# Windowed attention and a ternary FFN on one core: projections as two list steps, scores and maxima at places of their own

## The chip, the cores and the metric

One core of one Trainium2 chip. The metric is the device time of one execution of the whole kernel, in microseconds. TensorE is called PE, VectorE DVE, ScalarE ACT, GpSimd POOL and SyncE SP, as in the profile.

## The reference

A post-layernorm transformer layer over x of 16 x 512 x 256 (16 batch rows of 512 tokens), in float32:

```
qkv  = x @ Wqkv + bqkv                      16 heads of 16, blocks of 128 tokens
attn = softmax(q k^T / 16) v                each block sees itself and its neighbours, |kpos - qpos| <= 128
x1   = layernorm(x + attn @ Wout + bout)
Wq   = clip(round(W / (mean|W| + 1e-5)), -1, 1)       for W1 and W2
out  = layernorm(x1 + relu(x1 @ Wq1^T + b1) @ Wq2^T + b2)
```

## The kernel before, in words

The sixteen batch rows run through a software pipeline. `steps` (L209) calls each engine's `step` for row after row; while the attention of row b runs, the layer's second half (`POST`: ot, op, ln1, x1, x1t, f1, f2, ln2) of row b - 1 and the projections (qk, vp) of row b + 1 run beside it. Each row has four quads v of four heads. The order of the work is written out by hand: `SIDE[v]` (L54) is the list of side steps of quad v, and every engine walks it in that order, doing its part of each step.

- Attention comes in units, twelve of scores and twelve of maxima a quad (three for each head: blocks 1, 2, and 3 with 0). A score unit (`scores`, L504) is one or two matmuls of 384 or 2 x 256 columns into one of two banks `st`; ACT's `exp` (L765) reads it. A maxima unit (`max_scores`, L526) computes the same scores the other way round, for the quad two further on, into one of two banks `mx`; DVE's `row_max` (L923) reads it. Score units of quads 0 and 1 and maxima units of quads 2 and 3 use the lower 64 rows of PE's array, the others the upper 64, so that a score unit and a maxima unit can run side by side.
- `weave` (L108) sets where the units lie: two score and two maxima units in turn (s, m, s, m) make a run, six runs a quad, at one place inside a side step. Places are counted by `COST` (columns, places).
- Every projection and transposition has two halves (`in_halves`, L544; `transposes_in_halves`, L568): in the first, the array's lower rows write bank 0 and the upper ones bank 1 of a pair, then they swap. Before the second half PE waits on `s_half` until the first is complete. `passed` issues the units of a place.
- Side steps use two bank pairs in turn (`pairs`, L92). Before it writes, `pair_free` (L499) waits for the last reader: hid_lo of DVE after an f1 step, v_next of ACT after vp, DVE's addition (L1026) after f2, ACT's copy u (L825) after pv.
- nmt transposes the negated maxima (L603) for the next quad, pv (L613) multiplies the masked probabilities by v, ut (L626) transposes the result. POOL masks the probabilities (`mask`, L1091, four instructions after exp 5 and after exp 11), and pv of the next quad waits for it.
- `warm` (L490) issues matmuls whose results nobody reads ahead of some steps (`WARM`; `WARM_END` for the last row of the pipeline), each time a pair of 512 columns.
- ACT does its part of nmt, ot, pv and x1t ahead of the exps of that step, of all others behind them (L865 to L874). DVE follows `dve_order` (L184), in which `LAG` puts some parts behind later maxima.
- SP issues all transfers in the order of `TRANSFERS` (L76): a stack is six DMAs of 128 KB that lay out q and k (hi and lo parts) of a quad, x is the transposed input two rows on, residual the plain one, maxima the negated maxima, store half a result.

The lines of the helpers: L522 scores, L538 maxima, L563 all projections, L494 warm pairs, L583 ot and x1t, L960 qk_lo, L981 oT_lo, L1014 x1T_lo, L1019 hid_lo, L843 x1, L849 x1T_hi.

## Time and profile before

| | us |
|---|---|
| median of 3 runs | 1104.79 (1100.22 to 1110.8) |
| the profiled execution | 1103.1 |
| its span, first to last instruction | 1101.4 |
| PE busy in it | 997.7 |
| DVE busy in it | 846.3 |
| ACT, POOL busy in it | 621.7, 552.7 |
| mean granted clock of TensorE | 0.961 |

All durations come from one profiled execution; its time is 0.15% under the median of the runs, and the time outside the span is 1.7 us. PE's busy time is the union of modelled matmul intervals (a 512-column matmul shows about 0.4 us, and the next may start 0.23 us after it), so that starts are the better measure of how fast PE goes on. A clock of 1.00 means 2.4 GHz.

### The profile page before, as it was taken

How to read it: one execution, taken by the hardware profiler on the slowest of the kernel's cores; microseconds unless marked ns; L12 is line 12 of the kernel's file. 1: busy time of each engine (PE TensorE's matmuls, PEld its weight loads, DVE VectorE, ACT ScalarE, POOL GpSimd, SP SyncE). 2: the span in 40 equal slices, each digit the busy share in tenths (PEclk: the TensorE clock that was granted, in tenths of full speed). 3: DMA queues.
4: the chain of work that ended last, by engine and by line, in shares of the span. 5: the costliest groups of instructions: out<-in, count | busy, mean ns of one | idle time of the engine just before them, and what ended most of it. 6: DMA issues, size and time to landing. Idle time of an engine off the chain costs nothing.

```text
span 1101.4 us, 30158 instructions
## 1 busy us (share of the span) xinstructions
PE 997.7 (91%) x11408; PEld 780.5 (71%) x11408; DVE 846.3 (77%) x2965; ACT 621.7 (56%) x1275; POOL 552.7 (50%) x904
## 2 busy tenths in 40 slices
PE   5688998999999999999999899999999899998966
PEld 4465776777778677777778687777778677766755
DVE  3876888878798888879798887879788887867223
ACT  2355665747475565747476565747566574746411
POOL 2376355364645456374645456374655446354520
PEclk8678999999999999999999999999999999998988
DMA  5846435455364536556264536546254635541000
GB/s 115 162 68 82 60 63 97 67 90 86 54 97 69 88 55 95 77 80 97 41 103 66 96 51 98 79 74 103 42 97 67 97 56 79 79 68 33 11 11 20
DMA packets 57024, 81.92 MB, mean 74 GB/s; under 512 B 7712, under 2 KB 27696, under 8 KB 56880
## 3 DMA queue, kind: packets, MB, share of 16 engines
q1 hardware_dynamic: 56880, 80.00, 46.1%
q8 instruction: 91, 1.49, 0.7%
q14 instruction: 53, 0.43, 0.2%
HBM read 20.20 MB, written 8.39 MB: 26 GB/s over the span
## 4 chain that ended last, share of the span: by engine, by line
PE 60%; DVE 18%; ACT 9%; issue 7%; POOL 4%; DMA 1%; SPq 0%; DVEq 0%; POOLq 0%; ACTq 0%
PE shared L563 28%; PE shared L613 11%; PE st L522 9%; DVE mx L933 8%; PE mx L538 6%; ACT probs L780 4%; PE shared L494 2%; ACT x L843 2%; DVE hid_lo L1019 2%; PE shared L583 2%; ACT oT_x1T_hi L849 2%; DVE rmax L933 1%; POOL probs L1099 1%; DVE qk_lo L960 1%; POOL probs L1103 1%
## 5 line engine op out<-in xcount | busy, mean ns | idle before, releaser
L933 DVE CUSTOM_DVE_ANT_0 mx<-mx,band 128x384 f32<-128x384 f32 (+1 forms) x1024 | 478.8, 518 | 151.1 <-PE mx L538 145.9
L780 ACT ACTIVATE probs<-st 128x384 f32<-128x384 f32 (+1 forms) x768 | 365.1, 526 | 173.1 <-PE st L522 171.3
L1099 POOL TENSOR_SCALAR_AFFINE_SELECT probs<-probs 128x512 f32<-128x512 f32 (+1 forms) x256 | 127.4, 522 | 406.6 <-ACT probs L780 406.6
L538 PE MATMUL mx<-k_stack,q_stack 48*128 48x384 f32 (+1 forms) x1024 | 269.5, 344 | 14.8 <-DVE rmax L933 8.5
L522 PE MATMUL st<-q_stack,k_stack 50*128 50x384 f32 (+1 forms) x1024 | 243.9, 333 | 10.2 <-ACT probs L780 4.9
L522 PEld LDWEIGHTS st<-q_stack,k_stack 50*128 50x128 f32 x1024 | 167.7, 189 | 58.8 <-issue 31.0
L538 PEld LDWEIGHTS mx<-k_stack,q_stack 48*128 48x128 f32 x1024 | 170.1, 191 | 40.3 <-DVE rmax L933 27.3
L613 PE MATMUL shared<-probs,v_aug 128*32 128x384 f32 (+1 forms) x2048 | 164.9, 447 | 9.4 <-POOL probs L1103 7.2
L563 PE MATMUL shared<-w2q,hid_hi 64*128 64x256 f32 x1024 | 144.5, 290 | 0.3
L933 DVE DVE_READ_ACCUMULATOR2_ANT rmax<- 128x1 f32 x1024 | 144.6, 141 | 0.0
L563 PE MATMUL shared<-w2q,hid_lo 64*128 64x256 f32 x1024 | 136.0, 278 | 0.0
L613 PEld LDWEIGHTS shared<-probs,v_aug 128*32 128x32 f32 x2048 | 90.8, 112 | 56.4 <-issue 18.4
L1103 POOL TENSOR_SCALAR_AFFINE_SELECT probs<-probs 128x512 f32<-128x512 f32 (+1 forms) x256 | 127.1, 521 | 0.0
L563 PEld LDWEIGHTS shared<-w2q,hid_hi 64*128 64x128 f32 x1024 | 115.7, 185 | 2.0 <-PE shared L563 0.6
L563 PEld LDWEIGHTS shared<-w2q,hid_lo 64*128 64x128 f32 x1024 | 116.8, 185 | 0.0
L563 PE MATMUL shared<-oT_x1T_hi,w1q 64*128 64x512 f32 x512 | 112.3, 407 | 0.3
L563 PE MATMUL shared<-oT_x1T_lo,w1q 64*128 64x512 f32 x512 | 109.9, 400 | 0.0
L1019 DVE SCALAR_TENSOR_TENSOR hid_lo<-shared,hid_hi 128x512 fp32r<-128x512 f32 x128 | 82.1, 682 | 31.8 <-ACT hid_hi L856 31.8
L494 PE MATMUL shared<-wqkv_hi 64*128 64x512 f32 x596 | 95.2, 416 | 8.1 <-DVE qk_lo L960 4.4
L825 ACT ACTIVATE u<-shared 128x512 f32<-128x512 f32 x64 | 38.0, 594 | 101.9 <-PE shared L613 101.8
L856 ACT ACTIVATE hid_hi<-shared 128x512 fp32r<-128x512 f32 x128 | 69.6, 595 | 30.8 <-PE shared L563 30.4
L1169 POOL TENSOR_SCALAR x<-x,ln_mv,ln_rstd 128x256 f32<-128x256 f32 x60 | 73.3, 1227 | 3.2
(113 smaller groups left out, 1848.7 us busy)
## 6 DMA issues: line engine op xcount, KB each, us to landing
q_stack<-qk_hi SPq DMA_DIRECT2D x128, 128.0 KB, 4.0
k_stack<-qk_hi SPq DMA_DIRECT2D x128, 128.0 KB, 4.9
x_raw<-in_xT SPq DMA_DIRECT2D x16, 512.0 KB, 5.9
q_stack<-qk_lo SPq DMA_DIRECT2D x64, 128.0 KB, 5.6
k_stack<-qk_lo SPq DMA_DIRECT2D x64, 128.0 KB, 5.8
y<-in_x SPq DMA_DIRECT2D x16, 512.0 KB, 6.2
out<-x SPq DMA_DIRECT2D x32, 256.0 KB, 2.4
probs<-in_w2T SPq DMA_DIRECT2D x1, 1024.0 KB, 10.2
```

The costliest lines, as they stand in the source:

```text
L494: pe.matmul(out[i][:, 0:width], WQKV[0][rows, 0, 0:P], WQKV[0][rows, 1, 0:width], start=True, stop=True)
L522: mm = pe.matmul(PST[i % N_SCORE][:, col:col + n], SK[rows, hd, W * m:W * m + W], SQ[rows, hd, q0:q0 + n], start=True, stop=True)
L538: mm = pe.matmul(PMX[i % N_MAX][:, col:col + n], SQ[rows, hd, W * m:W * m + W], SK[rows, hd, k0:k0 + n], start=True, stop=True)
L563: mm = pe.matmul(out[k][:, cols], lhs(rows), rhs(rows), start=(swap == 0 and n == 0 and bias is None), stop=(swap == 1 and n == count - 1) ...
L613: mm = pe.matmul(out[0][32 * g:32 * g + 32, q0:q0 + width], VAUG[:, vq, m, g, :], PR[:, vq % 2, g // 2, lo:lo + width], start=(m == 0), st ...
L780: act.activation(PR[:, v % 2, g // 2, lo:lo + n], PST[i % N_SCORE][:, 0:n], ACT.Exp, scale=SCALE) \
L856: act.activation(HID[0][:, f, :], PG[:, 2 * k + i, :], ACT.Relu).then_inc(s_hh, 1)
L933: mx = dve.tensor_tensor_reduce(ps, ps, band, 1.0, -3e38, ALU.add, ALU.max, RMAX[:, g, m:m + 1])
L1019: dve.scalar_tensor_tensor(HID[1][:, f, :], PG[:, 2 * k + i, :], 0.0, HID[0][:, f, :].bitcast(F32), ALU.max, ALU.subtract).then_inc(s_hl, 1)
L1099: pool.affine_select(out=pr_before, in_=pr_before, compare_op=ALU.is_ge, fill=0.0, base=0, pattern=[[0, n], [1, W]], channel_multiplier=-1)
L1103: last = pool.affine_select(out=pr_after, in_=pr_after, compare_op=ALU.is_ge, fill=0.0, base=0, pattern=[[0, n], [-1, W]], channel_multipl ...
L1169: pool.tensor_scalar(X1[:, t, :], X1[:, t, :], MV2[:, t, 0:1], RS2[:, t:t + 1], ALU.subtract, ALU.mult).then_inc(s_o, 1)
```

## The change

Each step that works in halves stands twice in `SIDE`: `("start", step)` is its first half, the step's own name the second. The evacuations on ACT and DVE belong to the second. Both stand next to each other everywhere, so the matmuls of a step are the same as before. The lists differ otherwise in three places: vp stands ahead of f1 1, `("ut", 2)` behind xs and `("ut", 3)` at the end of quad 3, and x1 1 stands behind pv. Every score unit and every maxima unit has a position of its own (`SCORES_AT`, `MAXIMA_AT`, in thousandths of the quad's cost, pv counted as 5200 columns instead of 2500). Units at one place are issued scores first, then maxima. By these tables the units lie at 13, 11, 9 and 10 places of the four quads, where there were 6 in each.

ACT gets lags like DVE's: x1t's part comes behind the exps of its step. DVE's op lag is 2 (0 before), which leaves its order as it was. Two warm pairs are added ahead of `("start", "qk", 0)`; in the last row x1t has 16 instead of 14 and f1 0 none instead of 8. The wait of a quad's first score unit for the stack of the quad two further on goes, the wait of that quad's first maxima unit for it stays. `TRANSFERS` has another order. `pairs` now hands the two bank pairs out in turn by their use. `steps` runs one turn more, in which no step has a row.

The diff, cut to its core:

```diff
-    ["nmt", "pv", "ut", "ot", "op", ("ln1", 0), ("ln1", 1), ("ln1", 2), ("ln1", 3)],
-    [("qk", 0), ("x1", 0), ("x1", 1), "nmt", "pv", ("x1", 2), "ut", ("x1", 3), "x1t", ("qk", 1), ("f1", 0)],
-    [("f1", 1), "vp", ("f1", 2), ("f1", 3), "nmt", "pv", "ut", ("xs", 0), ("xs", 1)],
-    [("f2", 0), ("ln2", 0), "xr", ("ln2", 1), "nmt", "pv", "ut", ("f2", 1), ("ln2", 2), ("ln2", 3)],
+    ["nmt", "pv", ("ut", 0), ("start", "ot"), "ot", ("start", "op"), "op", ("ln1", 0), ("ln1", 1), ("ln1", 2),
+     ("ln1", 3)],
+    [("start", "qk", 0), ("qk", 0), ("x1", 0), "nmt", "pv", ("x1", 1), ("ut", 1), ("x1", 2), ("x1", 3),
+     ("start", "x1t"), "x1t", ("start", "qk", 1), ("qk", 1), ("start", "f1", 0), ("f1", 0)],
+    [("start", "vp"), "vp", ("start", "f1", 1), ("f1", 1), ("start", "f1", 2), ("f1", 2), ("start", "f1", 3),
+     ("f1", 3), "nmt", "pv", ("xs", 0), ("xs", 1), ("ut", 2)],
+    [("start", "f2", 0), ("f2", 0), ("ln2", 0), "xr", ("ln2", 1), "nmt", "pv", ("start", "f2", 1), ("f2", 1),
+     ("ln2", 2), ("ln2", 3), ("ut", 3)],
 ]
 
-COST = {"qk": (6144, 12), "vp": (6144, 24), "op": (6144, 24), "ot": (1024, 8), "x1t": (1024, 8), "ut": (512, 4),
-        "f1": (4096, 8), "f2": (8192, 32), "nmt": (0, 0), "pv": (2500, 1)}
+HALF_COST = {"qk": (3072, 6), "vp": (3072, 12), "op": (3072, 12), "ot": (512, 4), "x1t": (512, 4),
+             "f1": (2048, 4), "f2": (4096, 16)}
+COST = {"ut": (512, 4), "nmt": (0, 0), "pv": (5200, 1)}
...
-HALVED = {"qk", "vp", "op", "ot", "x1t", "f1", "f2"}
...
-RUN = 2
-RUNS_AT = (0.95, 0.93)
-TRANSFERS = (('stack', 3), ('maxima', 0), ('x', 0), ('stack', 0), ('maxima', 1), ('stack', 1), ('residual', 0), ('maxima', 2), ('maxima', 3), ('stack', 2), ('store', 0), ('store', 1))
-
-LAG = {"ln1": 3, "ln2": 0, "qk": 0, "ut": 0, "ot": 1, "x1t": 0, "f1": 0, "op": 0, "f2": 0}
+SCORES_AT = ((201.86, 241.86, 488.2, 488.2, 572.67, 572.67, 631.93, 691.93, 771.43, 771.43, 930.43, 930.43),
+             (168.94, 168.94, 370.2, 378.2, 537.72, 562.72, 701.04, 726.04, 789.62, 814.62, 922.49, 922.49),
+             (47.43000000000001, 87.43, 279.19, 384.19, 400.22, 400.22, 511.54999999999995, 526.55, 681.2, 681.2, 871.11, 871.11),
+             (191.17, 191.17, 245.68, 245.68, 513.4100000000001, 520.4100000000001, 690.22, 698.22, 820.42, 860.42, 928.28, 936.28))
+MAXIMA_AT = ((161.86, 216.86, 448.2, 463.2, 532.67, 540.67, 591.93, 651.93, 731.43, 791.43, 890.43, 938.43),
+             (143.94, 143.94, 338.2, 370.2, 529.72, 529.72, 693.04, 726.04, 789.62, 814.62, 922.49, 922.49),
+             (47.43000000000001, 87.43, 279.19, 384.19, 400.22, 415.22, 511.54999999999995, 526.55, 681.2, 681.2, 911.11, 919.11),
+             (191.17, 231.17, 285.68, 285.68, 545.4100000000001, 553.4100000000001, 690.22, 698.22, 820.42, 860.42, 928.28, 936.28))
+TRANSFERS = (("maxima", 0), ("stack", 3), ("maxima", 1), ("x", 0), ("stack", 0), ("stack", 1), ("residual", 0),
+             ("maxima", 2), ("stack", 2), ("maxima", 3), ("store", 0), ("store", 1))
+DVE_LAG = {"ln1": 3, "ln2": 0, "qk": 0, "ut": 0, "ot": 1, "x1t": 0, "f1": 0, "op": 2, "f2": 0, "vp": 0}
+WARM = {("start", "ot"): 4, ("start", "op"): 4, ("ut", 0): 2, ("ut", 1): 2, ("ut", 2): 2, ("ut", 3): 2,
+        ("start", "x1t"): 2, ("start", "qk", 0): 2}
+WARM_END = {("start", "x1t"): 16}
+WARM_UP = 14
+FILLED = set()
+ACT_LAG = {"nmt": -1, "ot": -1, "pv": -1, "x1t": 0, ("ut", 0): -1, ("ln2", 1): 0, ("ln1", 3): -1, ("x1", 3): 0}
 N_PAIRS = 2
-WARM_END = {"x1t": 14, ("f1", 0): 8}
-WARM_UP = 14
-WARM = {"ot": 4, "op": 4, "ut": 2, "x1t": 2}
...
-        total = sum(COST.get(name_of(s), (0, 0))[0] for s in SIDE[v])
-        at, starts = 0, []
-        for s in SIDE[v]:
-            starts.append(at)
-            at += COST.get(name_of(s), (0, 0))[0]
-        place, last = {}, -1
-        runs = range(0, UNITS, RUN)
-        where = [(i + RUNS_AT[0] * RUN) / UNITS * total * RUNS_AT[1] for i in runs]
-        for k, s in enumerate(SIDE[v]):
-            if name_of(s) in HALVED:
-                cost, places = COST[name_of(s)]
-                middle = starts[k] + cost / 2
-                free = [n for n in range(last + 1, len(where))]
-                if free:
-                    last = min(free, key=lambda n: abs(where[n] - middle))
-                    place[last] = (k, places // 2)
-        slot = [[] for _ in SIDE[v]]
-        for n, i in enumerate(runs):
-            if n in place:
-                k, p = place[n]
-            else:
-                k = max(k for k, s in enumerate(SIDE[v]) if starts[k] <= where[n] and COST.get(name_of(s), (0, 0))[0])
-                cost, places = COST[name_of(SIDE[v][k])]
-                p = min(int((where[n] - starts[k]) / cost * places), places - 1)
-            slot[k] += [(p, kind, u) for u in range(i, i + RUN) for kind in ("scores", "max")]
-        out.append(slot)
-        order = [u for units in slot for _, kind, u in units if kind == "max"]
-        assert order == list(range(UNITS))
+        costs = [cost_of(s) for s in SIDE[v]]
+        starts = [sum(c for c, _ in costs[:k]) for k in range(len(costs))]
+        total = sum(c for c, _ in costs)
+        put = {}
+        for kind, table in (("scores", SCORES_AT), ("max", MAXIMA_AT)):
+            for i in range(UNITS):
+                pos = table[v][i] * total / 1000
+                k = max(k for k in range(len(costs)) if costs[k][0] and (starts[k] <= pos or k == 0))
+                put[kind, i] = (k, min(int((pos - starts[k]) / costs[k][0] * costs[k][1]), costs[k][1] - 1))
+            for k, s in enumerate(SIDE[v]):
+                if name_of(s) in HALF_COST and (k, 0) not in [put[kind, i] for i in range(UNITS)]:
+                    near = sorted(range(UNITS), key=lambda i: abs(table[v][i] * total / 1000 - starts[k]))[0]
+                    if abs(table[v][near] * total / 1000 - starts[k]) <= 1300 and \
+                            all(put[kind, i] <= (k, 0) for i in range(near)) and \
+                            all(put[kind, i] >= (k, 0) for i in range(near + 1, UNITS)):
+                        put[kind, near] = (k, 0)
+        out.append([sorted(((p, kind, i) for (kind, i), (k, p) in put.items() if k == n), key=lambda u: (u[0], u[1] != "scores", u[2]))
+                    for n in range(len(costs))])
+        for kind in ("scores", "max"):
+            assert [i for units in out[-1] for _, what, i in units if what == kind] == list(range(UNITS))
...
+def turn_of(v, step):
...
+    if name == "nmt":
+        return (0, v + 1) if v < 3 else (1, 0)
+    turn = v if name == "pv" else step[1]
+    return (-1, (turn - 1) % QUADS) if turn == 0 or turn > v else (0, turn - 1)
...
+def act_order(v):
+    out, late, exps = [], [], 0
+    def due(now):
+        while late and late[0][0] <= now:
+            out.append(("side", late.pop(0)[1]))
+    for step, woven in zip(SIDE[v], WOVEN[v]):
+        lag = lag_of(ACT_LAG, step)
+        if lag < 0:
+            due(UNITS + 100)
+            out.append(("side", step))
+        for _, kind, i in woven:
+            if kind == "scores":
+                out.append(("exp", i))
+                exps += 1
+                due(exps)
+        if lag >= 0:
+            late.append((exps + lag, step))
+            due(exps)
+    due(UNITS + 100)
+    return out
...
-                    pe.wait_ge(s_nmin[v], 16 * b + 16)
-                    if v < 2 or stages(at)[2]:
-                        pe.wait_ge(s_stk[(v + 2) % 4], 96 * (b + v // 2) + 96)
...
+            def exchange(passed):
+                passed()
+                pe.wait_ge(s_half, halves[0])
+            def one_half(out, terms, filled, passed, second, ready=None, bias=None):
 
 
                 count = len(terms[0])
-                if bias is not None:
+                if second:
+                    exchange(passed)
+                elif bias is not None:
                     for k, rows in enumerate((LOWER, UPPER)):
                         pe.matmul(out[k][:, :], bias(rows), ONES_R[rows, :], start=True, stop=False, skip_group_check=True)
-                for swap in range(2):
-                    if swap:
+                for n in range(count):
+                    if n > 0 or not second:
                         passed()
-                        halves[0] += 2
-                        pe.wait_ge(s_half, halves[0])
-                    for n in range(count):
-                        if n > 0 or not swap:
-                            passed()
-                        if ready is not None and not swap:
-                            ready(n)
-                        for rows, k in ((LOWER, swap), (UPPER, 1 - swap)):
-                            cols, lhs, rhs = terms[k][n]
-                            mm = pe.matmul(out[k][:, cols], lhs(rows), rhs(rows), start=(swap == 0 and n == 0 and bias is None),
-                                           stop=(swap == 1 and n == count - 1), skip_group_check=True)
-                            if n == count - 1:
-                                mm.then_inc(filled if swap else s_half, 1)
-
-            def transposes_in_halves(out, block, filled, passed, ready=None):
-
-
-                for swap in range(2):
-                    if swap:
+                    if ready is not None and not second:
+                        ready(n)
+                    for rows, k in ((LOWER, second), (UPPER, 1 - second)):
+                        cols, lhs, rhs = terms[k][n]
+                        mm = pe.matmul(out[k][:, cols], lhs(rows), rhs(rows), start=n == 0 and not second and bias is None,
+                                       stop=n == count - 1 and bool(second), skip_group_check=True)
+                        if n == count - 1:
+                            mm.then_inc(filled if second else s_half, 1)
+                            halves[0] += not second
...
-                    for step, woven in zip(SIDE[v], WOVEN[v]):
-                        row = row_of(v, step, at)
-                        before = name_of(step) in ("nmt", "ot", "pv", "x1t")
-                        if row is not None and before:
-                            side_work(v, step, b, *row, at)
-                        for _, kind, i in woven:
-                            if kind == "scores" and attn:
-                                exp(b, v, i, at)
-                        if row is not None and not before:
-                            side_work(v, step, b, *row, at)
+                    for kind, what in act_order(v):
+                        if kind == "exp":
+                            if attn:
+                                exp(b, v, what, at)
+                        else:
+                            row = row_of(v, what, at)
+                            if row is not None:
+                                side_work(v, what, b, *row, at)
```

## Rows read from the trace of the kernel before

**Rows 1.** The page's busy table: busy us, share of the span, instructions
```profile
PE 997.7 (91%) x11408; PEld 780.5 (71%) x11408; DVE 846.3 (77%) x2965; ACT 621.7 (56%) x1275; POOL 552.7 (50%) x904
```

**Rows 2.** Windows: stretch and its us, busy us of each engine (instructions), clock, DMA, GB/s
```profile
482.45:544.77 62.32, 58.71 (x708) 46.59 (x708) 51.80 (x185) 38.25 (x79) 33.19 (x56) 1.00 0.52 79
...
1049.00:1101.00 52.00, 36.00 (x328) 27.79 (x324) 16.52 (x39) 8.88 (x16) 6.70 (x14) 0.81 0.05 16
```

**Rows 3.** Waits over the span: who <- for whom, us in total, times, longest
```profile
PE shared L603 <- DVE neg_max L944: 15.6, 16, 1.9
...
PEld shared L563 <- DVE hid_lo L1019: 13.5, 14, 1.0
```

**Rows 4.** Timeline of DVE and PE around vp: start, us, idle before <- releaser
```profile
511.57 1.41 DVE L960 SCALAR_TENSOR_TENSOR qk_lo<-shared,bqk,qk_hi 128x512 fp32r<-128x512 f32 x2 [0.16 <-ACT qk_hi L804]
...
514.94 1.27 DVE L1019 SCALAR_TENSOR_TENSOR hid_lo<-shared,hid_hi 128x512 fp32r<-128x512 f32 x2
...
515.34 0.40 PE L563 MATMUL shared<-oT_x1T_lo,w1q 64*128 64x512 f32 x2
516.27 0.39 PE L563 MATMUL shared<-wqkv_hi,xT_hi 64*128 64x256 f32 x2 [0.53 <-DVE hid_lo L1019]
```

**Rows 5.** Timeline of PE: quad 3's ut, then the start of a row
```profile
475.05 0.63 PE L494 MATMUL shared<-wqkv_hi 64*128 64x512 f32 x4
475.52 0.41 PE L626 MATMUL shared<-identity,u 64*128 64x64 f32 x8
475.73 0.37 PE L563 MATMUL shared<-w2q,hid_hi 64*128 64x256 f32 x2
...
482.45 0.41 PE L603 MATMUL shared<-identity,neg_max 128*32 128x128 f32 x2 [0.94 <-DVE neg_max L944]
483.37 0.96 PE L613 MATMUL shared<-probs,v_aug 128*32 128x256 f32 x12 [0.51 <-POOL probs L1103]
```

**Rows 6.** Timeline of DVE and POOL in the same stretch
```profile
482.32 0.68 DVE L1026 TENSOR_TENSOR x<-shared,x 128x512 f32<-128x512 f32 x1
...
481.38 0.99 POOL L1099 TENSOR_SCALAR_AFFINE_SELECT probs<-probs 128x512 f32<-128x512 f32 x2 [1.88 <-ACT probs L780]
```

**Rows 7.** Timeline of ACT and PE around x1t and qk 1
```profile
506.31 1.09 ACT L849 ACTIVATE oT_x1T_hi<-shared 128x512 fp32r<-128x512 f32 x2 [1.11 <-PE shared L583]
...
507.84 0.44 PE L522 MATMUL st<-q_stack,k_stack 50*128 50x384 f32 x1
...
508.33 0.44 PE L522 MATMUL st<-q_stack,k_stack 50*128 50x384 f32 x1
```

**Rows 8.** Windows: the stretch from oT_lo on; timeline of PE at ut 1
```profile
490.19:505.05 14.86, 13.72 (x162) 10.84 (x160) 14.17 (x53) 10.65 (x23) 6.48 (x16) 1.00 0.71 106
...
503.44 0.73 PE L494 MATMUL shared<-wqkv_hi 64*128 64x512 f32 x4 [0.32 <-DVE qk_lo L960]
```

**Rows 9.** Timeline of ACT: x1 2 and x1 3
```profile
504.13 1.07 ACT L843 ACTIVATE x<-y,ln_neg_mean_rstd,ln_rstd 128x256 f32<-128x256 f32 x2
```

**Rows 10.** Timeline of PE: a run of units in f1 0; op's end
```profile
511.32 0.42 PE L563 MATMUL shared<-oT_x1T_lo,w1q 64*128 64x512 f32 x2
...
511.97 0.43 PE L563 MATMUL shared<-oT_x1T_hi,w1q 64*128 64x512 f32 x2
...
496.49 0.39 PE L563 MATMUL shared<-xT_hi,wqkv_hi 64*128 64x512 f32 x1
496.60 0.28 PE L563 MATMUL shared<-wout_lo,oT_x1T_hi 64*128 64x256 f32 x1
```

**Rows 11.** Timeline of SP's queue; DMA issues: count, KB each, us to landing
```profile
501.39 1.20 SPq L420 DMA_DIRECT2D q_stack<-qk_hi  x2
...
x_raw<-in_xT SPq DMA_DIRECT2D x16, 512.0 KB, 5.9
...
k_stack<-qk_lo SPq DMA_DIRECT2D x64, 128.0 KB, 5.8
```

**Rows 12.** Timeline of PE in the tail: f1 0's warm pairs
```profile
1067.74 3.58 PE L494 MATMUL shared<-wqkv_hi 64*128 64x512 f32 x16 [2.04 <-DVE oT_x1T_lo L1014]
```

More of the change, by code:

```diff
@@ L181, in max_quad, with lag_of @@
     return (1, v - 2) if nxt else None
+def lag_of(lags, step):
+    return lags.get(step, lags.get(name_of(step), 0))
 def dve_order(v):
@@ L192, in dve_order @@
     for step, woven in zip(SIDE[v], WOVEN[v]):
-        while late and (any(name_of(s) == NEEDS.get(name_of(step)) for _, s in late)
-                        or name_of(step) in USES_BANKS and sum(name_of(s) in USES_BANKS for _, s in late) >= N_PAIRS):
+        while late and (any(name_of(s) == NEEDS.get(name_of(whole(step))) for _, s in late)
+                        or name_of(whole(step)) in USES_BANKS and sum(name_of(s) in USES_BANKS for _, s in late) >= N_PAIRS):
             out.append(("side", late.pop(0)[1]))
@@ L202, in dve_order @@
         after = late[-1][0] + 1 if late and name_of(late[-1][1]) == name_of(step) == "ln2" else 0
-        late.append((max(maxima + LAG.get(name_of(step), 0), after), step))
+        late.append((max(maxima + lag_of(DVE_LAG, step), after), step))
         due(maxima)
@@ L206, in dve_order @@
     return out
+def act_order(v):
[18 more added lines that the diff above has]
+    return out
 def steps(step):
[L211 removed]
+    for row in range(-2, B + 2):
         step(row, row)
@@ new lines, in half_of_transposes @@
+            def half_of_transposes(out, block, filled, passed, second, ready=None):
+                if second:
+                    exchange(passed)
+                for t in range(TB):
+                    if t > 0 or not second:
+                        passed()
+                    if ready is not None and not second:
+                        ready(t)
+                    for rows, k in ((LOWER, second), (UPPER, 1 - second)):
+                        col = P * t + rows.start
+                        mm = pe.transpose(out[k][:, col:col + 64], block(rows, t, k), IDN[rows, rows])
+                        if t == TB - 1:
+                            mm.then_inc(filled if second else s_half, 1)
+                            halves[0] += not second
@@ L591, in side_work @@
             def side_work(v, step, b, dr, vq, at, passed):
+                second = int(name_of(step) != "start")
+                k = PAIR[at, v, step]
+                whole_step = step
+                step = whole(step)
                 name = name_of(step)
@@ L631, in side_work @@
                     c = step[1]
-                    if c == 0:
+                    if c == 0 and not second:
                         pe.wait_ge(s_xh, 2 * r + 2)
@@ L646, in side_work @@
                     left, right, col = (XT, WQKV, 2 * D) if name == "vp" else (OT, WOUT, 0)
-                    if first:
+                    if first and not second:
                         pe.wait_ge(s_wsplit_h, 2 if name == "vp" else 3)
@@ L675, in side_work @@
                     p = step[1]
-                    if first and p == 0:
+                    if first and p == 0 and not second:
                         pe.wait_ge(s_quant_d, 3)
@@ L735, in step @@
                         row = row_of(v, step, at)
-                        if row is not None and name_of(step) in COST:
+                        if row is not None and cost_of(step) != (0, 0) or row is not None and step == "nmt":
                             side_work(v, step, b, *row, at, passed)
+                        elif row is None and (at == 0 or at == -1 and v > 1) and name_of(whole(step)) in FILLED:
+                            cost, count = HALF_COST[name_of(whole(step))]
+                            out = pair_free(PAIR[at, v, step], b)
+                            for _ in range(count):
+                                passed()
+                                warm(out, 1, cost // count // 2)
                         units(1000)
@@ L786, in side_work @@
                 first = at is not None and at + dr == 0
-                k = PAIR.get((v, step))
+                k = PAIR.get((at, v, step))
                 if name == "xs":
@@ L950, in side_work @@
                 first = at is not None and at + dr == 0
-                k = PAIR.get((v, step))
+                k = PAIR.get((at, v, step))
                 if step == ("xs", 1) and first:
```

141 lines of the change are left out of this document (76 added, 65 removed).

## The prediction

> **What bounds the kernel now.** I read the page's busy table first, then one steady batch row cut out by windows, then the table of waits, and last the instructions of each engine around the longest waits. PE is busy 997.7 us, DVE 846.3 us [rows 1]. The kernel does the same thing sixteen times: the negated-maxima transposes that open a row start at 482.45 and again 62.32 us later. In that stretch PE is busy 58.71 us and DVE 51.80 us at a granted clock of 1.00; the last 52 us of the span have a clock of 0.81 [rows 2]. So the row period is PE's, with DVE at 83% close behind. The reader should see that "busy" hides waits on PE: a step's few long stalls come from one partner at a time. The table of waits gives them, each about once a row: the negated maxima's transposes wait for DVE (15.6 us in all, 16 times) and weight loads of side work for DVE's hid_lo (13.5 us, 14 times) [rows 3].
>
> **The change, part by part.** Matmuls, evacuations and masks are the same in number. What moves is their order, and where the 96 units a row (48 of scores, 48 of maxima) lie. I cost each per row and multiply by 15 rows that have a full partner.
>
> *vp before f1 1 (quad 2).* Today two f1 steps follow each other, and vp, third, needs the bank pair of f1 0. DVE reads that pair (hid_lo) only from 514.94 to 516.2, behind the maxima. PE's last f1 pair starts at 515.34, a 512-column pair takes 0.23 us, vp starts at 516.27: 0.70 us lost [rows 4]. Afterwards vp stands first and needs qk 1's pair, which DVE leaves at 512.98 (two instructions from 511.57, 1.41 us) [rows 4], just before f1 0 ends at about 513.0; f1 1 then needs f1 0's pair at 516.2, when vp (24 pairs of 0.115 us and two runs of units, 3.2 us) ends, so 0.1 us stays. What is late next is DVE: f1 1 now holds four maxima units (0.5 to 0.8 us each) before its evacuation, three f1 steps follow closely, and f1 3 waits for f1 1's. Placing DVE's durations one behind the other I get hid_lo at about 521.3 against f1 3's turn at 521.6: level. I take -0.6 (ends: -0.9, if the shorter bank waits of f1 2 go too; 0, if f1 3 or the maxima's banks take the wait over).
>
> *ut 3 behind f2 1 (quad 3).* Today, behind pv, two warm pairs (475.05, 0.47 us until ut) and ut (0.21 us) stand on PE before f2 1 at 475.73: 0.68 us. At the row's end PE idles: 0.94 us before the transposes at 482.45 and 0.51 us before pv at 483.37 [rows 5]. The new place is inside that idle time. But two things follow it. The last score units go from place 10 to 11 and 12 of the half (a place is 0.115 us), so the last exp, the four masks (from 481.38, 0.99 us for each two) and pv come 0.23 us later. And the transposes now share their bank pair with f2 1, so they queue behind DVE's addition at 482.32 (0.68 us) instead of ahead of it: ready at about 483.1 rather than 482.4, still 0.3 us before the masks allow pv [rows 5, 6]. Gain 0.68 - 0.23 = 0.45. I take -0.45 (ends -0.68 and 0; the latter if DVE's maxima run 0.5 us later than now).
>
> *ScalarE's x1T evacuation behind exp 4; units of qk 1 on own places.* Today ScalarE takes x1T (506.31, 1.09 us) before the exps of the units in the same step, and qk 1's next score units find both banks full: s6 starts at 507.84, s7 at 508.33, where 384 columns at 2.4 GHz (0.16 us) would separate them [rows 7]: 0.33 us lost, and I estimate as much ahead of s6. But the maxima there wait for DVE too (x1T_lo). Half goes: -0.3 (ends -0.6, 0).
>
> *x1 1 behind pv, and two warm pairs before qk 0.* DVE works without a pause from oT_lo (490.19) past qk_lo, to 505.05: 14.17 us busy in 14.86; ut's warm pairs start at 503.44, after 0.32 us idle that qk_lo ends [rows 8]. Four maxima now stand nearer to op's start, DVE begins them up to 0.2 us earlier and loses 0.2 of the 0.7 us that it idles there, so ut 1 can come 0.4 us sooner. Against it, ScalarE has three x1 left (0.55 each) behind exp 3 where it had two (504.13, 1.07 us) [rows 9], so x1t's last transposes come 0.5 us later, less what the two maxima units in x1t's first half cover. The new warm pairs cost 0.47 us on PE by [rows 5], below nothing only if they keep a clock that is at 1.00 already. They lie in a stretch where DVE is the slower: they eat slack first. Together I take +0.15 (ends -0.4, +0.9).
>
> *Forty-three places instead of twenty-four.* A run of 896 columns (0.37 us at 2.4 GHz) between two 512-column pairs makes start-to-start 0.65 us (511.32 to 511.97) where 0.23 + 0.37 is 0.60: 0.05 us a place [rows 10]. Nineteen more places cost up to 0.95. Today each score unit runs beside its maxima unit, on the other half of the array's rows; now many stand alone and rely on the two halves drifting apart. That they do drift: qk 0's first matmul starts at 496.49, before the last wout_lo one at 496.60, which stands ahead of it in the program [rows 10]. So I take +0.3 (ends 0, +0.95 without the loss of the rival below).
> The Trainium skill (TensorE: Matmul & The Clock Gate, Part 3) says matmuls start and end strictly in program order, "strict FIFO, no reordering". The trace's 0.11 us the wrong way round is against it. By the page the row would gain about 1.6 us from eight places alone, by the trace none of that.
>
> *SyncE's order and the removed wait.* Nothing on PE waits for a stack in a steady row, so the removed wait is worth 0. Moving x ahead of stack 0 is not free: stack 0's six DMAs are issued from 501.39 on, 0.6 us each, and the last kind lands 5.8 us after issue; x lands in 5.9 [rows 11]. Behind maxima 1 and x they start at about 503.6; the last is issued at 506.7 and lands at 512.5 or somewhat later; vp's first maxima unit wants it at 513.2. I take 0 (ends 0, +3).
>
> *Tail.* Eight warm pairs of f1 0 go, two come to x1t. Sixteen matmuls, they took 3.58 us in the tail, behind 2.04 us of idle time [rows 12]: at 0.45 us a pair that is the lower clock level, and without them the steps behind would run part of that time at that level. -1 (ends -3.4, +2).
>
> Sum: -0.6 - 0.45 - 0.3 + 0.15 + 0.3 = -0.9 a row; a further -0.1 for op's maxima, which no longer starve DVE, makes -1.0; times 15 is -15, tail -1: -16. The profiled execution took 1103.1 us (span 1101.4), 1.7 under the shown median of 1104.8, well inside the shown runs. 1103.1 - 16 = 1087.
>
> **Rivals.** *(A) More goes.* If PE's short bank waits shrink as well (PE's busy time counts them: at s6 and s7 alone they are 0.6 us), the lower ends of the first three parts hold: -2.2 a row, 1069. For it: every quad has two exps and two maxima in a run against two banks each. Against: DVE needs 51.8 of 62.3 us whatever the order. Chance 0.17.
> *(B) Given back.* The stall of vp turns up at f1 3 or ut 2, since DVE's work in quad 2 is unchanged and only bunched: first part 0, sum -0.4 a row, 1097 to 1103, say 1099. For it: four maxima units in f1 1. Chance 0.19.
> *(C) Lost side-by-side running (slower).* Eight places put two score units before two maxima units. If the second pair can't start until the last score matmul has, the first unit (0.16 to 0.27 us, say 0.2) is paid each time, 1.6 us, and single units on the lower rows hold both halves, about 0.9: -1.0 + 2.5 = +1.5 a row, 1103 + 22 = 1125. It decides from 1.0 us a row, five of the eight places. The page's rule is this rival; the pair at 496.49 speaks against it. Chance 0.08.
> *(D) Stack 0 late (slower).* If x and the stack transfer one after the other in full, the last landing is 514.6 or later, 1.4 us and more behind vp's unit; at 2.6 us a row: 1103 + 15 x 1.6 = 1127. It decides from a landing 1.0 us after 513.2. Against: the 5.8 us already hold the queueing of a sixth DMA behind five. Chance 0.06.
>
> **How the numbers follow.** Forecast -1.0 a row: 0.50, between 1078 and 1096. With A 0.17, B 0.19, C 0.08, D 0.06. Range 1068 to 1107: it takes in A to its middle and B, and leaves C and D out, and half of A's far side. A measurement tells about 1% (11 us) from no change. Faster by over 1% (under 1093.7): 0.47 of the forecast's, A's 0.17, 0.02 of B's: 0.66. Within: 0.03 + 0.16 + 0.01 = 0.20. Slower: C and D with 0.01 of B: 0.14.
>
> **What would show it.** Row period 61.3 us between transposes of quad 0 (62.32 now). No wait of vp for hid_lo, at most 0.1 us at f1 1. f2 1 right behind pv's units; idle before pv of quad 0 down by some 0.2 us with ut 3 in front. s7 behind s6 by under 0.2 us in qk 1. PE busy up by 0.4 us a row for the warm pairs. Wrong if k_stack appears as a releaser of mx (D); if score runs followed by maxima runs start one behind the other (C); if hid_lo or v_next releases f1 3 or ut 2 for over 0.4 us (B).

## The result and the profile after

The changed kernel takes 1162.3 us (median of 4 runs, 1155.6 to 1173.0) against 1102.5 for the one before: ratio 1.0503, 95% interval [1.0444, 1.0562]. It is slower by 5%. Forecast were 1087 and faster; the case that came true is rival D, stack 0 late, to which I had given a chance of 0.06 and 1127 us. The profiled execution is the slowest of the four (1173.0, mean granted clock 0.931; the others 0.939 to 0.941), so its rows hold some more loss of clock than the median execution, and the ratio is that of the other three.

The page of the changed kernel, its head and its chain (shares of the span):

```profile
span 1171.3 us, 30226 instructions
...
PE 1050.6 (90%) x11460; PEld 836.8 (71%) x11460; DVE 859.3 (73%) x2965; ACT 631.8 (54%) x1275; POOL 552.6 (47%) x904
...
PEclk8576999998998989999999999999899999999987
...
PE 63%; DMA 13%; DVE 11%; SPq 5%; issue 4%; ACT 3%; POOL 0%; DVEq 0%; POOLq 0%; ACTq 0%
PE shared L645 32%; DMA k_stack<-qk_lo 12%; PE shared L698 10%; PE st L601 8%; PE mx L617 8%; DVE mx L1023 5%; SPq L500 4%; PE shared L576 1%; PE shared L688 1%; PE shared L637 1%; PE shared L663 1%; DVE rmax L1023 1%; DVE oT_x1T_lo L1071 1%; DVE x L1116 1%; ACT oT_x1T_hi L926 1%
```

PE's share hardly moved (91% in [rows 1]), and would tell nothing. The chain does: one kind of DMA, k_stack<-qk_lo, holds 12% of the span. The table of waits says who waits for it, and how often (who <- for whom, us in total, times, longest):

```profile
PEld mx L617 <- DMA k_stack<-qk_lo: 47.6, 16, 4.6
...
PE mx L617 <- DMA k_stack<-qk_lo: 43.2, 16, 4.3
...
PEld shared L688 <- DVE x L1116: 19.0, 14, 1.5
```

Sixteen times, once a row. One of them in the timelines of SP's queue and of PE (start, us, idle before <- releaser):

```profile
543.73 0.66 SPq L544 DMA_DIRECT2D q_stack<-neg_maxT  x1
544.43 0.41 SPq L531 DMA_DIRECT2D x_raw<-in_xT  x1
544.94 1.21 SPq L500 DMA_DIRECT2D q_stack<-qk_hi  x2
546.19 1.25 SPq L500 DMA_DIRECT2D k_stack<-qk_hi  x2
547.48 0.60 SPq L500 DMA_DIRECT2D q_stack<-qk_lo  x1
548.12 0.63 SPq L500 DMA_DIRECT2D k_stack<-qk_lo  x1
...
555.05 0.34 PE L601 MATMUL st<-q_stack,k_stack 50*128 50x384 f32 x1
558.07 0.44 PE L617 MATMUL mx<-k_stack,q_stack 48*128 48x384 f32 x1 [2.68 <-DMA k_stack<-qk_lo]
```

The row starts at 524.17, with the transposes of quad 0. SP issues stack 0 from 544.94, at +20.8, as forecast (+21.1). Its last DMA is issued at 548.12, at +23.9, and vp's first maxima unit asks for it at about +30.9, as forecast (+30.7). But the unit starts at +33.9. The DMA issues of that stretch (count, KB each, us from issue to landing) say why: the last one takes 9.9 us and lands at 558.0, where the same DMA of the kernel before, issued at 504.55, took 5.8:

```profile
k_stack<-qk_lo SPq DMA_DIRECT2D x1, 128.0 KB, 9.9
```

In that stretch the DMA engines are full, or nearly, for eight microseconds; the windows of the changed kernel (share of the 16 engines and GB/s last) above, of before ([rows 11]'s stretch) below:

```profile
544.00:548.00 4.00, 3.76 (x45) 2.82 (x46) 3.46 (x14) 3.23 (x7) 0.36 (x2) 1.00 0.62 158
548.00:552.00 4.00, 4.00 (x40) 3.21 (x38) 3.58 (x13) 3.23 (x8) 3.88 (x4) 1.00 1.08 100
552.00:556.00 4.00, 3.39 (x35) 2.44 (x31) 3.80 (x13) 3.81 (x9) 1.93 (x5) 1.00 0.88 113
```

```profile
502.00:506.00 4.00, 3.54 (x51) 2.46 (x45) 3.44 (x14) 3.20 (x8) 1.06 (x3) 1.00 0.82 125
506.00:510.00 4.00, 3.81 (x40) 2.79 (x38) 3.49 (x12) 2.97 (x7) 1.65 (x4) 1.00 0.75 82
```

Below I call the time from one row's first transposes of negated maxima in quad 3 to the next row's the period, median of twelve rows from the third on. It was 62.30 before and is 66.94 now: 4.64 us more, where the wait is 2.7. Windows of single rows of the changed kernel, from one row's transposes in quad 0 to the next, say what the rest is (clock third from the end):

```profile
189.47:253.78 64.31, 60.28 (x712) 48.40 (x713) 52.69 (x184) 38.90 (x79) 33.20 (x56) 1.00 0.49 76
321.14:390.12 68.98, 62.76 (x712) 50.87 (x712) 52.77 (x184) 38.85 (x79) 33.42 (x56) 0.95 0.46 71
524.17:590.87 66.70, 61.88 (x713) 49.86 (x713) 52.71 (x184) 38.98 (x79) 33.20 (x56) 0.97 0.50 74
926.99:991.85 64.86, 60.14 (x713) 48.38 (x713) 52.72 (x184) 38.90 (x79) 33.20 (x56) 1.00 0.51 76
991.85:1053.93 62.08, 59.99 (x713) 48.34 (x713) 52.50 (x184) 37.85 (x77) 30.86 (x55) 1.00 0.46 71
```

PE waits for stack 0 for 1.89, 3.92, 2.68 and 2.45 us in the first four, and not at all in the last. That row loads no x, and its stack 0 lands 6.2 us after its last issue. Where the clock stays at 1.00 (first and fourth), a row is 2.2 and 2.8 us longer than the last one, about its wait. The second and third are 6.9 and 4.6 us longer, 3.0 and 1.9 us more than their wait, and their clock is lower; in the third it is 0.50 from 559.8 to 563.2, right behind the wait that ends at 558.07. Before, the clock was 1.00 in the steady row of [rows 2]. So two things are in the loss, the wait and the clock behind it.

### The profile page after: what moved, and what is told of

Read it like the earlier page. It is cut to its first block, busy times and chain, and to the rows that moved or that the text cites. A ratio compares the mean times of both kernels' runs of the same rounds, so it can differ in the third digit from the quotient of the medians.

```text
span 1171.3 us, 30226 instructions
## 1 busy us (share of the span) xinstructions
PE 1050.6 (90%) x11460; PEld 836.8 (71%) x11460; DVE 859.3 (73%) x2965; ACT 631.8 (54%) x1275; POOL 552.6 (47%) x904
## 4 chain that ended last, share of the span: by engine, by line
PE 63%; DMA 13%; DVE 11%; SPq 5%; issue 4%; ACT 3%; POOL 0%; DVEq 0%; POOLq 0%; ACTq 0%
PE shared L645 32%; DMA k_stack<-qk_lo 12%; PE shared L698 10%; PE st L601 8%; PE mx L617 8%; DVE mx L1023 5%; SPq L500 4%; PE shared L576 1%; PE shared L688 1%; PE shared L637 1%; PE shared L663 1%; DVE rmax L1023 1%; DVE oT_x1T_lo L1071 1%; DVE x L1116 1%; ACT oT_x1T_hi L926 1%
## 5 line engine op out<-in xcount | busy, mean ns | idle before, releaser
L872 ACT ACTIVATE probs<-st 128x384 f32<-128x384 f32 (+1 forms) x768 | 377.2, 528 | 215.3 <-PE st L601 209.3
L617 PE MATMUL mx<-k_stack,q_stack 48*128 48x384 f32 (+1 forms) x1024 | 287.6, 350 | 59.0 <-DMA k_stack<-qk_lo 43.2
L601 PE MATMUL st<-q_stack,k_stack 50*128 50x384 f32 (+1 forms) x1024 | 270.1, 338 | 4.3 <-ACT probs L872 2.7
L617 PEld LDWEIGHTS mx<-k_stack,q_stack 48*128 48x128 f32 x1024 | 183.1, 197 | 92.4 <-DMA k_stack<-qk_lo 47.6
L601 PEld LDWEIGHTS st<-q_stack,k_stack 50*128 50x128 f32 x1024 | 177.6, 194 | 53.0 <-issue 27.1
L645 PE MATMUL shared<-w2q,hid_lo 64*128 64x256 f32 x1024 | 143.0, 281 | 0.0
L645 PE MATMUL shared<-oT_x1T_hi,w1q 64*128 64x512 f32 x512 | 116.7, 420 | 0.4
L645 PE MATMUL shared<-oT_x1T_lo,w1q 64*128 64x512 f32 x512 | 113.9, 404 | 0.0
L645 PEld LDWEIGHTS shared<-w2q,hid_lo 64*128 64x128 f32 x1024 | 112.2, 185 | 0.0
L576 PE MATMUL shared<-wqkv_hi 64*128 64x512 f32 x648 | 104.8, 412 | 2.6 <-DVE y L1079 1.4
L1109 DVE SCALAR_TENSOR_TENSOR hid_lo<-shared,hid_hi 128x512 fp32r<-128x512 f32 x128 | 82.3, 684 | 22.2 <-ACT hid_hi L948 20.8
```

The lines of the kernel that those rows point to most:

```text
L576: pe.matmul(out[i][:, 0:width], WQKV[0][rows, 0, 0:P], WQKV[0][rows, 1, 0:width], start=True, stop=True)
L601: mm = pe.matmul(PST[i % N_SCORE][:, col:col + n], SK[rows, hd, W * m:W * m + W], SQ[rows, hd, q0:q0 + n], start=True, stop=True)
L617: mm = pe.matmul(PMX[i % N_MAX][:, col:col + n], SQ[rows, hd, W * m:W * m + W], SK[rows, hd, k0:k0 + n], start=True, stop=True)
L645: mm = pe.matmul(out[k][:, cols], lhs(rows), rhs(rows), start=n == 0 and not second and bias is None, stop=n == count - 1 and bool(second) ...
L872: act.activation(PR[:, v % 2, g // 2, lo:lo + n], PST[i % N_SCORE][:, 0:n], ACT.Exp, scale=SCALE) \
L1109: dve.scalar_tensor_tensor(HID[1][:, f, :], PG[:, 2 * k + i, :], 0.0, HID[0][:, f, :].bitcast(F32), ALU.max, ALU.subtract).then_inc(s_hl, 1)
```

## The experiments

**First: is it the order of transfers?** Theory 1: x's 512 KB, queued right ahead of stack 0, make it late. Theory 2: units at places of their own lose their running side by side (rival C). Theory 3: maxima 1 in front of stack 0 delays it.

`e1_old_transfers`, the changed kernel with

```diff
-TRANSFERS = (("maxima", 0), ("stack", 3), ("maxima", 1), ("x", 0), ("stack", 0), ("stack", 1), ("residual", 0),
-             ("maxima", 2), ("stack", 2), ("maxima", 3), ("store", 0), ("store", 1))
+TRANSFERS = (('stack', 3), ('maxima', 0), ('x', 0), ('stack', 0), ('maxima', 1), ('stack', 1), ('residual', 0),
+             ('maxima', 2), ('maxima', 3), ('stack', 2), ('store', 0), ('store', 1))
```

> The changed kernel with the order of transfers of before. Theory 1 (stack 0 lands late because x is queued right ahead of it): the wait of mx for k_stack, 2.7 us a row in the changed kernel, is gone, no clock dips in the middle, row period 62.1 us as in the one row of the changed kernel that loads no x, time 1098 to 1104. Theory 2 (score and maxima units at places of their own lose their running side by side): time stays at 1125 or more, row period at 64 us or more without any DMA wait. Theory 3 (maxima 1 ahead of stack 0 delays it): as theory 1 here.

Measured: 1101.3 us, ratio 0.9919 [0.9894, 0.9944] to the kernel before, period 62.10. The whole 5% is the order of transfers.

`e2_x_before_maxima1`:

```diff
-TRANSFERS = (("maxima", 0), ("stack", 3), ("maxima", 1), ("x", 0), ("stack", 0), ("stack", 1), ("residual", 0),
+TRANSFERS = (("maxima", 0), ("stack", 3), ("x", 0), ("maxima", 1), ("stack", 0), ("stack", 1), ("residual", 0),
```

> The changed kernel with x moved ahead of maxima 1 and nothing else, so that maxima 1 still stands ahead of stack 0. Theory 1: x is then issued some 15 us earlier, stack 0's last DMA lands about 6 us after its issue instead of 8.7, near row start + 31, and mx waits under 0.5 us a row: 1098 to 1110. Theory 3: stack 0 still starts 1.9 us late behind maxima 1 and at least 1.5 us a row of waiting stay: 1130 or more. Theory 2: 1125 or more.

Measured: 1102.5 us, 0.9926 [0.9899, 0.9954], period 62.10. Maxima 1 may stand ahead of stack 0; theory 3 falls. One swap of neighbours in a list is worth 60 us.

In the list of before, too, x stood right ahead of stack 0. What counts is when SP comes to it: the kernel issues the list in order and has SP wait, ahead of each transfer, for what it needs. Before, x stood behind maxima 0 (issued at 492.06) and was issued 10.3 us into the row of [rows 11], 8.6 us ahead of stack 0:

```profile
492.75 0.40 SPq L449 DMA_DIRECT2D x_raw<-in_xT  x1
```

Behind maxima 1, which is ready at 543.73 in the row shown above, it is issued 20.3 us into the row, 0.5 us ahead of stack 0. In e2 it is back at 9.7 to 10.3 us, and stack 0's last DMA lands 4.8 to 5.9 us after its issue (steady rows).

`e3_before_new_transfers`, the kernel before with nothing but the changed `TRANSFERS`:

> The kernel before with the changed order of transfers and nothing else. Its quad 2 asks for stack 0 at row start + 31.9 us (the changed kernel at + 30.9), and behind maxima 1 and x it lands at about + 33.9. Theory 1: mx waits about 2 us a row for k_stack, plus what the clock loses: 1130 to 1150. Theory 2: 1100 to 1106, since the order of transfers has nothing to do with it.

Measured: 1169.3 us, 1.0503 [1.0452, 1.0554], period 66.73. Its wait sits on the score unit, since that kernel still has the wait which the change removed:

```profile
PE st L523 <- DMA k_stack<-qk_lo: 50.2, 16, 5.3
```

The direction is theory 1's, the size is 20 us above what I expected of it: the period is 4.43 us longer than the 62.30 of before, of which about 3.1 are wait (50.2 us over sixteen rows) and about 1.3 come behind it. Its steady rows at a clock of 1.00 take 64.6 to 65.0 us, the others 66.2 to 69.8. The order alone slows the old kernel just as much, so the loss is independent of all the rest of the change.

`e4_x_after_stack0`:

```diff
-TRANSFERS = (("maxima", 0), ("stack", 3), ("maxima", 1), ("x", 0), ("stack", 0), ("stack", 1), ("residual", 0),
+TRANSFERS = (("maxima", 0), ("stack", 3), ("maxima", 1), ("stack", 0), ("x", 0), ("stack", 1), ("residual", 0),
```

> The changed kernel with x moved behind stack 0 and nothing else. Stack 0 then starts 0.5 us earlier and x's 512 KB are shared with the end of stack 0 at most, but x now runs into stack 1, which has 9 us of slack. Theory 1: mx's wait for k_stack falls to under 1 us a row: 1100 to 1115. Theory 3: 1.5 us a row stay: 1125 or more. Theory 2: 1125 or more.

Measured: 1099.4 us, 0.9909 [0.988, 0.9938], period 62.10, just as with x far ahead. This is the base of what follows; its page:

```profile
span 1097.5 us, 30226 instructions
...
PE 1017.5 (93%) x11460; PEld 808.1 (74%) x11460; DVE 856.1 (78%) x2965; ACT 632.4 (58%) x1275; POOL 552.7 (50%) x904
...
PEclk9578999999999999999999999999999999998988
```

**Second: how much of the loss is the clock?** `g2_filled_wait` leaves the changed order alone and gives PE work to do while it would wait:

```diff
-        ("start", "x1t"): 2, ("start", "qk", 0): 2}
+        ("start", "x1t"): 2, ("start", "qk", 0): 2, ("start", "vp"): 12}
```

> The changed kernel as it stands, x ahead of stack 0, with twelve more warm pairs (2.8 us) ahead of vp, where PE would otherwise stand still for stack 0 some 2.5 us later. If part of the 5 us that a row has lost is the clock that falls after the wait, the clock stays at 1.00, the period becomes about 65.0 and the time about 1142, although PE has more work. If the clock has no part in it, the added 2.8 us take the wait's place at best: period 67, time 1162 or more.

Measured: 1136.2 us, 1.0288 [1.0234, 1.0343], period 64.70. 384 matmuls more, 26 us less than the changed kernel's 1162.3. Its page:

```profile
PE 1052.6 (93%) x11844; PEld 834.9 (74%) x11844; DVE 860.0 (76%) x2965; ACT 632.1 (56%) x1275; POOL 552.4 (49%) x904
...
PEclk9588999999999999999999999999999999999988
```

No dip to "8" is left in the steady part of this line, where the changed kernel had four. But the run does not price the clock, as I had meant it to, because in it stack 0 is no longer late. Its issue, landing time and PE's timeline in one row (start 501.34):

```profile
525.29 0.59 SPq L500 DMA_DIRECT2D k_stack<-qk_lo  x1
...
k_stack<-qk_lo SPq DMA_DIRECT2D x1, 128.0 KB, 6.8
...
531.63 3.02 PE L576 MATMUL shared<-wqkv_hi 64*128 64x512 f32 x24
534.95 0.34 PE L617 MATMUL mx<-k_stack,q_stack 48*128 48x384 f32 x1
```

It lands 6.8 us after its issue, at +30.8, about when the changed kernel asks for it (+30.9), and 2.8 us before this one does. In the steady rows that load x it takes 6.3 to 7.9 us, in the changed kernel's 9.1 to 11.3, with the same order and the same issue times. So the 2.60 us that g2's period has above 62.10 are the price of the added pairs (12 at 0.23 us are 2.8), and not stack 0's lateness. Why it lands sooner stays open: x itself takes 5.0 us instead of 7.1 (medians), and it has landed before the added pairs start.

How much of the loss is the clock is therefore read from the changed kernel itself. Its profiled execution is 73.7 us longer than e4's (1173.0 against 1099.3). Its waits for stack 0 make 43.2 us, those of e4 1.9, so about 41 us are wait and about 32 come behind it, some 2.1 us a row. The median execution is 11 us shorter; if its waits were the same, the part behind them is about 22 us there, an estimate. The Trainium skill (TensorE: Matmul & The Clock Gate, "Why this matters for your kernels") warns of idle gaps between bursts of matmuls as a cause of throughput drops. The trace agrees in ten of the twelve steady rows that load x, with waits of 2.1 to 4.0 us and a clock of 0.95 to 0.98; in the other two, with waits of 1.9 and 2.45 us, it stays at 1.00.

**Third: where did my expected 1.0 us a row go?** With the transfers mended the period is only 0.20 below before. Each run takes one part of the change back on the base of e4 (62.10).

`f4_vp_after_f11`: `("start", "f1", 1), ("f1", 1)` ahead of `("start", "vp"), "vp"` again.

> The same base with f1 1 ahead of vp again. If the wait of vp for f1 0's bank pair was removed for good, as forecast, 0.6 us a row come back: period 62.7. If it was given back elsewhere in quads 1 and 2, 62.1 to 62.3. The stretch from the transposes of quad 1 to those of quad 2 was 25.44 before and is 24.86 in the base; I expect it at 25.4 and the period at 62.6.

Measured: period 63.09, 1117.0 us (0.99 us a row dearer). The stretch from quad 1's to quad 2's transposes is 25.80 against 24.82. The old wait is back in the table of waits:

```profile
PEld shared L645 <- DVE hid_lo L1109: 10.8, 14, 0.8
```

`f1_no_warm_qk`:

```diff
-        ("start", "x1t"): 2, ("start", "qk", 0): 2}
+        ("start", "x1t"): 2}
```

> The changed kernel with x behind stack 0 (row period 62.10, 1099.4), and without the two warm pairs ahead of qk 0. If PE leads between the transposes of quads 0 and 1 (17.37 us), the 0.47 us come off in full: period 61.6. If DVE's unbroken stretch there sets the pace, nothing comes off: 62.0 to 62.1. I expect the latter for the most part: 61.9.

Measured: period 61.67, 1095.9 us. 0.43 of the 0.47 us come off. I had expected half of that at most: PE then does wait for DVE at ut 1, but the 0.37 us of it are hardly longer than the 0.32 of [rows 8]:

```profile
564.70 0.73 PE L576 MATMUL shared<-wqkv_hi 64*128 64x512 f32 x4 [0.37 <-DVE qk_lo L1050]
```

`f3_units_in_turn`:

```diff
-key=lambda u: (u[0], u[1] != "scores", u[2]))
+key=lambda u: (u[0], u[2], u[1] != "scores"))
```

> The same base with the units of one place issued in turn (score, maxima, score, maxima) as before the change, instead of scores first; eight places have two of each. If score units ahead of maxima units lose their running side by side, the period falls by 1.6 us to 60.5. If the halves of the array drift apart freely, it stays within 0.2 of 62.10. I expect 62.0.

Measured: period 61.50, 1090.7 us, 0.9907 [0.9878, 0.9937] to a kernel before that ran at 1101.5 beside it (1110.4 beside the base, so that periods are compared, not ratios). 0.60 us a row, between my two alternatives. The same four units of f1 2, first in the base (scores first), then in turn:

```profile
583.68 0.59 PE L645 MATMUL shared<-oT_x1T_lo,w1q 64*128 64x512 f32 x2
583.91 0.51 PE L601 MATMUL st<-q_stack,k_stack 50*128 50x384 f32 x2
584.11 0.51 PE L617 MATMUL mx<-k_stack,q_stack 48*128 48x384 f32 x2
584.36 0.49 PE L645 MATMUL shared<-oT_x1T_hi,w1q 64*128 64x512 f32 x2
584.69 0.40 PE L645 MATMUL shared<-oT_x1T_lo,w1q 64*128 64x512 f32 x2
```

```profile
580.18 0.34 PE L601 MATMUL st<-q_stack,k_stack 50*128 50x384 f32 x1
580.18 0.34 PE L617 MATMUL mx<-k_stack,q_stack 48*128 48x384 f32 x1
580.35 0.34 PE L601 MATMUL st<-q_stack,k_stack 50*128 50x384 f32 x1
580.36 0.34 PE L617 MATMUL mx<-k_stack,q_stack 48*128 48x384 f32 x1
580.53 0.40 PE L645 MATMUL shared<-oT_x1T_hi,w1q 64*128 64x512 f32 x2
580.77 0.39 PE L645 MATMUL shared<-oT_x1T_lo,w1q 64*128 64x512 f32 x2
```

From the first unit to the second projection pair: 0.78 us scores first, 0.59 in turn. Scores first, the first maxima unit starts 0.20 us behind the first score unit instead of beside it. So the halves do not wait for each other in full (that would be 0.2 us at each of eight places, 1.6), but the second kind does start late, 0.075 us a place on average.

`f2_ut3_back`: `("ut", 3)` behind quad 3's `"pv"` instead of at its end.

> The same base with ut 3 put back behind pv of quad 3, ahead of f2 1 (its units shift with it by two places of f2 1). If moving it brought 0.45 us a row, as forecast, the period becomes 62.5; if the wait for f2 1's bank pair (1.40 us of gap before the transposes of quad 0, releaser the DVE addition) ate most of it, 62.1 to 62.3. I expect 62.25.

Measured: period 62.06. Moving ut 3 brought nothing. (Its time, 1107.4, holds two rows of 65.9 and 63.8 us that the base doesn't have; in the early one the clock was at 0.89 between 100 and 160 us, so I go by the period.) The reason stands in the changed kernel's timelines of PE, DVE and POOL at the start of a row:

```profile
522.55 0.42 PE L711 MATMUL shared<-identity,u 64*128 64x64 f32 x8
524.17 0.41 PE L688 MATMUL shared<-identity,neg_max 128*32 128x128 f32 x2 [1.20 <-DVE x L1116]
524.48 0.96 PE L698 MATMUL shared<-probs,v_aug 128*32 128x256 f32 x12
...
523.43 0.68 DVE L1116 TENSOR_TENSOR x<-shared,x 128x512 f32<-128x512 f32 x1
...
522.49 0.99 POOL L1189 TENSOR_SCALAR_AFFINE_SELECT probs<-probs 128x512 f32<-128x512 f32 x2 [1.76 <-ACT probs L872]
523.44 0.99 POOL L1193 TENSOR_SCALAR_AFFINE_SELECT probs<-probs 128x512 f32<-128x512 f32 x2
```

ut 3 does stand inside the idle time, and DVE's addition does release the transposes. But the masks end at 524.43, the addition at 524.11. Counted from the last f2 pair (521.97; 481.23 before), that is 0.38 and 0.37 us later than before, since the last scores and maxima lie later, and pv waits for the masks whatever stands in front. In [rows 5] pv started 2.14 us after that pair; here it does so 2.51 us after it, with ut in between: 0.37 later, where I had 0.23. With ut 3 put back, it starts 2.20 us after it, and from quad 3's transposes to that pair it is 9.09 us instead of 8.77 (medians of ten rows). So the move takes 0.32 us off PE's way to the last f2 pair, not 0.68, and pv's delay of 0.31 gives it back. Where the rest of the 0.68 goes stays open.

`g4_x1T_ahead_of_exp4`: `"x1t": -1` in `ACT_LAG`.

> The changed kernel with x behind stack 0 (62.10) and ScalarE's x1T evacuation put back ahead of the exps of that step. Forecast: the new place is worth 0.3 us a row, so the period becomes 62.4. If DVE's x1T_lo sets qk 1's units anyway, or the evacuation that comes earlier pays for the exps that come later, within 0.1 of 62.10. I expect 62.2.

Measured: period 62.15, 1099.4 us. The new place of x1T's evacuation is worth 0.05 us, not 0.3.

**Last: a version that beats both.** `g1_three_mended` joins e4, f1 and f3:

> The changed kernel with x behind stack 0, units of a place in turn, and no warm pairs ahead of qk 0, together. If the three are independent, the period is 62.10 - 0.43 - 0.60 = 61.07 us and the time 1099.4 - 15 x 1.03 = about 1084. If DVE's stretch takes part of it back, 61.3 and about 1088. I expect 61.1, 1085.

Measured: 1088.4 us, 0.9855 [0.9792, 0.9917], period 61.22. Of the 1.03 us, 0.88 add up; ut 1 now waits for DVE.

`g3_last_units_earlier`, on top of it, with quad 3's positions of units 8 to 11:

```diff
-820.42, 860.42, 928.28, 936.28)
+810.0, 840.0, 897.0, 905.0)
```

> As g1_three_mended, with the last two score and maxima units of quad 3 two to three places earlier in f2 1. The gap ahead of the transposes of quad 0 (1.4 us) waits for DVE's addition behind the last maxima; three places are 0.35 us. If the maxima set that, the gap shrinks and the period falls by 0.2 to 0.3 us against g1; if the masks or f2 1's end set it, no change (within 0.05).

Measured: 1085.1 us, 0.9822 [0.977, 0.9874], period 60.98. The gap ahead of the weight load of the transposes falls from 1.34 to 0.87 us, and 0.24 arrive in the period. In its table of waits that wait is down from 18.9 us in g1:

```profile
PEld shared L688 <- DVE x L1116: 12.4, 14, 1.1
```

It is the fastest kernel of the study, 1.8% faster than before.

## Why the prediction was wrong

**The step that failed** is "SyncE's order and the removed wait": "I take 0 (ends 0, +3)". I had the issue times right to 0.4 us, the need right to 0.2, and put the landing at "512.5 or somewhat later", some 30 us into the row; it was 33.8. The figure behind it, 5.8 us from issue to landing, was right for a stack 0 that had the engines to itself: before, x was issued 8.6 us ahead of it and had landed (5.9 us) when its first DMA was issued. It moves with what is queued ahead: behind x it is 9.1 to 11.3 in the steady rows of the changed kernel (and 6.3 to 7.9 in g2, for which no run gives a reason). The step also misnames what was moved: x stood ahead of stack 0 already, and it was maxima 1, now ahead of x, that brought it up against stack 0. Rival D had the reason and 2.6 us a row, close to the 2.7 of wait (43.2 us in sixteen rows). I had argued against it that 5.8 us "already hold the queueing of a sixth DMA behind five"; true, but x adds four DMAs' worth of bytes in front of them. A slack of under 1 us against a transfer that I had just moved should have given D more than any other case.

**The clock was no term at all.** Rival D ended at 1127, the kernel at 1162, so even the right mechanism missed by 35 us. Some 12 of them are gains that D counted on (1.0 us a row) and that did not come (0.20). The rest is what follows a PE standing still: about 22 us in the median execution and 32 in the profiled one, a third to two fifths of the loss. The waits of 0.94 and 0.51 us in [rows 5] left the clock at 1.00; waits of 2.1 to 4.0 us did not, and those of 1.9 and 2.45 us did.

**A sum.** Rival A's -2.2 a row adds up the three lower ends alone. With the other terms of the forecast (+0.15, +0.3, -0.1) it is -1.8 a row, some 1075 instead of 1069.

**The other steps, by the runs** (us a row; forecast, then measured):

| step | forecast | measured |
|---|---|---|
| vp ahead of f1 1 | -0.6 | -0.99 (f4) |
| ut 3 behind f2 1 | -0.45 | 0.04 (f2) |
| x1T behind exp 4 | -0.3 | -0.05 (g4) |
| warm pairs ahead of qk 0 | with x1 1 and ut 1: +0.15 | +0.43 (f1) |
| more places, scores first | +0.3 | +0.60 for scores first alone (f3) |
| x right ahead of stack 0 | 0 | +4.84 (e4), of which about 2.7 wait and 2.1 clock (the changed kernel's rows) |

Without the last row the measured ones make +0.03; the period says -0.20, so that -0.23 belong to what no run took apart (the single places themselves, x1 1, maxima nearer to op). My sum for this was -1.0. The vp step was right and undersized, a little beyond the lower end of its range (-0.9). It was not given back: no wait for hid_lo at f1 3 shows. For ut, pv was held by the masks, which end 0.32 us behind the addition whatever stands on PE. For x1T, I had named DVE as a second partner of qk 1's units; g4 fits that, but no row here shows it. I had named both partners and then still taken half and all of the gain. Rival C fell as worked out, since the halves drift, but over a third of its first term is there (0.60 of 1.6).

The slack that I assumed for the warm pairs was not PE's. 14.17 of 14.86 us of DVE busy [rows 8] looked like a stretch that DVE paces, yet taking PE work out of it shortened it by the whole of that work: PE was close to the pace at the same time.

The tail's term (-1) is of the right sign: from the last row's first transposes to PE's end it is 121.8 us in e4 against 124.7 before. That stretch holds more than the warm pairs, so their share stays open. x1 1's new place was not tried alone.

## What to carry to other kernels

Before moving a transfer, write down when its successors in the queue are needed and how many bytes now stand ahead of them; a median from issue to landing is only valid for the neighbours it was measured with. Look also at what SP stops for: a transfer that needs no data of the kernel starts late when it stands behind one that does. When a stall on PE is longer than those that the steady clock has been seen to survive, add what the clock loses, which here was half of the stall and more. Filling such a stall with matmuls went with 26 us less here, but in that run the transfer was early too, so that what the filling alone brings is not shown. Where two partners release a step within a few tenths of a microsecond, taking one away is worth the difference between them, and not the wait.

## What I had not expected of the hardware

- A stack's last DMA lands 9.9 us after its issue behind 512 KB of x, instead of 5.8 (the engines' share is 1.08 and 0.88 in the eight microseconds behind it), while x behind the stack costs nothing that the period shows (62.10 either way). In g2 the same DMA in the same queue takes 6.8 us, and nothing here says why.
- A wait of 2.7 us once in a row costs 4.84 in the profiled execution, since the clock falls behind it in ten of twelve steady rows. With 384 matmuls more, whose results nobody reads, stack 0 lands in time, the clock stays at 1.00, and the kernel is 26 us faster.
- Two score matmuls ahead of two maxima matmuls, on different halves of the array, cost about 0.08 us against the same four in turn (0.19 in the place shown): the halves drift apart, as the pair in [rows 10] says, but not at once.
